# Buffers that outlive a stage: the first q and k, and the first y and inverses, loaded in the stage before

## The chip, the cores and the metric

The kernel runs on one core of one Trainium2 chip. Its engines are TensorE (PE, with its weight loads shown apart as PEld), VectorE (DVE), ScalarE (ACT), GpSimd (POOL) and SyncE (SP), which here issues nearly all transfers; ACT issues a few. The metric is the device time of one execution in microseconds. The time of the kernel before is the median of three executions.

## The reference

A transformer over x of shape (2, 2048, 256), 16 heads of 16:

```python
x = x + attn_a(layernorm(x))    # softmax times a causal decay table, then @ W_proj
x = x + ffn(layernorm(x))       # binarised weights, gelu, 256 -> 1024 -> 256
x = x + attn_b(layernorm(x))    # plain causal softmax, @ Wo + bo, then a layernorm with gamma, beta
x = x + ffn(layernorm(x))       # the same ffn again
```

Each attention forms q, k and v of every head, softmax(q k^T / 4) under a causal mask, and its product with v. `attn_a` multiplies the softmax by decay weights that depend on the distance of the two positions.

## The kernel before

The program is six stages, one behind the other: `setup` (signs and constants), `projections` named `qkv_a`, `attention` named `att_a`, `dense` named `mid` (projection of att_a, the ffn, and q, k, v of the second attention), `attention` named `att_b`, and `dense` named `end`. Each stage is a block: all engines meet at its end, its semaphores are cleared, and its buffers are given back. What one stage hands to the next goes through scratch tensors in DRAM: `qk` and `v` into an attention, `y` and `inverse` (the reciprocal softmax sums) into a dense stage. A stage's end waits for its own stores (the last `wait_ge` lines of its sync program).

A chunk is 512 positions, four (NC) for each of two batches; dense stages number them G = 0 to 7. An attention works on eight groups g of four heads, each with chunks c = 0 to 3.

**Attention.** `kop` and `qop` hold k and q of two groups (parities). Rows 0 to 63 of a chunk are four loads each of 16 rows, 128 KB (`load`, lines 616 to 632); rows 64 to 127 are padding, written by memsets (`pad`, line 601): VectorE fills the four chunks of `qop` of the first group and only then runs its PLAN (line 742), GpSimd fills the others. The q of group 0 is loaded by ACT (line 705), its k by SP (line 622). Then comes `va` (v, line 632). PLAN (`attention_plan`) is one list for all engines. It merges two streams by computed positions: items "M" (TensorE forms a score block in `pm`, line 829; VectorE takes its row maximum, lines 759 and 763) and items "S" (scores again, line 842; ScalarE takes exp, line 718), followed by "PO" and "PV" (sums and products with v). M runs ahead of S by a lead of 0.38 or 0.45 of a group. "MC" copies the maxima into row 64 of `qop` (line 652), "O" copies an output chunk out and gathers its sums (`scol`, line 661), and "SU" takes their reciprocal (line 809) and stores it. "L" items load the next group's q and k. Every engine takes its items strictly in the order of PLAN, and `pm` has four banks.

**Dense.** PLAN (`dense_plan`) is again one list. "Y": VectorE multiplies `y` by `inverse` (line 1324). "P": TensorE projects it (line 1179), VectorE adds x or bias. "S": moments and normalisation. In `end`, "A" and "N" add x and normalise once more. "X" transposes, "H" and "O" are the ffn. PLAN begins Y0, P0, S0, Y1, P1, S1, X0, H in `mid`, and Y0, P0, S0, Y1, A0, N0, P1, S1, X0, A1, N1, Y2, H in `end`. SP loads y(0), in `end` then bo, gamma and beta (line 1047), then y(1) and x(1), in `mid` then the weights; ACT loads the projection's weights, x(0) and the two sign matrices of 1 MB (lines 1244 to 1247). A y load is four transfers, two of y and two of inverse, 256 KB each.

## Time and profile before

| | us |
|---|---|
| median of three runs | 2675.54 (2669.0 to 2676.61) |
| profiled execution, its own time | 2671.95 |
| its span | 2670.2 |

By the timeline the stages of the profiled execution are:

| stage | from | to |
|---|---|---|
| setup | 0 | 34.0 |
| qkv_a | 34.0 | 147.3 |
| att_a | 147.3 | 1139.7 |
| mid | 1139.7 | 1466.0 |
| att_b | 1466.0 | 2413.7 |
| end | 2413.7 | 2670.2 |

Times in the rows are microseconds from the start of the span, unless marked ns. A timeline row is: start, duration, engine, source line, operation, output<-input, shapes, count, and in brackets the idle time of that engine before it and what released it. SPq and ACTq are the issue of a transfer by that engine, not the transfer.

### The profile page before, as it was taken

To read this page: it belongs to the slowest core of one execution; us is meant where nothing else is said; L and a number is where in the kernel's file an instruction comes from. 1 tells how busy PE (TensorE), PEld (TensorE's weight loads), DVE (VectorE), ACT (ScalarE), POOL (GpSimd) and SP (SyncE) were. 2 spreads that over 40 slices of the span, in tenths; PEclk is the share of its full clock that TensorE was granted. 3 is DMA by queue.
4 is the path that set the end of the run, shared out by engine and by line. 5 is a ranking of instruction groups with operands and counts; after the bars stand their busy time and mean duration, and the time that the engine had idled before them with its cause. 6 is when DMAs were issued, how large, how long until landed. Compare 5 with 4: busy or idle time off the path is not lost. (4 is left out here: it accounts for less than half of the span.)

```text
span 2670.2 us, 43926 instructions
## 1 busy us (share of the span) xinstructions
PE 2396.0 (90%) x13600; PEld 1367.6 (51%) x13600; DVE 1962.1 (73%) x4834; ACT 1499.8 (56%) x3293; POOL 1054.0 (39%) x1274
## 2 busy tenths in 40 slices
PE   4969999999999999859996899999999999992887
PEld 2544545555454545346764455555555555532666
DVE  5677888878888888337653988888888878833887
ACT  1218677776868777614331266666666666670233
POOL 0037778788787778813211301010010110103552
PEclk8969999999999999979998699999999999996999
DMA  4684243351615330053323644261542615004210
GB/s 150 255 145 59 37 55 51 45 73 18 85 26 66 46 50 10 10 164 115 130 98 123 88 65 62 30 85 30 66 61 30 85 26 70 10 9 140 77 50 32
DMA packets 158806, 188.69 MB, mean 71 GB/s; under 512 B 65520, under 2 KB 89584, under 8 KB 157808
## 3 DMA queue, kind: packets, MB, share of 16 engines
q1 hardware_dynamic: 153840, 175.91, 33.5%
q10 hardware_dynamic: 4736, 9.96, 1.9%
q8 instruction: 113, 1.85, 0.3%
q14 instruction: 117, 0.96, 0.2%
HBM read 114.37 MB, written 69.99 MB: 69 GB/s over the span
## 5 line engine op out<-in xcount | busy, mean ns | idle before, releaser
L688 POOL TENSOR_TENSOR att_a_wd<-att_a_wt,decay 128x256 f32<-128x256 f32 (+3 forms) x896 | 754.4, 872 | 208.5 <-PE att_a_po L864 120.5
L718 ACT ACTIVATE att_b_wt<-att_b_ps 128x512 f32<-128x512 f32 (+3 forms) x1280 | 592.3, 540 | 325.5 <-PE att_b_ps L842 323.7
L759 DVE TENSOR_REDUCE att_a_mpart<-att_a_pm 128x1 f32<-128x512 f32 x768 | 508.8, 686 | 115.9 <-PE att_a_pm L829 110.8
L759 DVE TENSOR_REDUCE att_b_mpart<-att_b_pm 128x1 f32<-128x512 f32 x768 | 503.5, 685 | 95.4 <-PE att_b_pm L829 93.7
L829 PE MATMUL att_a_pm<-att_a_kop,att_a_qop 128*128 128x512 f32 (+3 forms) x1280 | 510.8, 425 | 45.5 <-DMA att_a_kop<-qk 19.1
L718 ACT ACTIVATE att_a_wt<-att_a_ps 128x512 f32<-128x512 f32 (+3 forms) x896 | 433.0, 511 | 207.2 <-PE att_a_ps L845 145.0
L829 PE MATMUL att_b_pm<-att_b_kop,att_b_qop 128*128 128x512 f32 (+3 forms) x1280 | 486.7, 400 | 29.7 <-DMA att_b_kop<-qk 18.4
L842 PE MATMUL att_b_ps<-att_b_qop,att_b_kop 128*128 128x512 f32 (+3 forms) x1280 | 453.9, 384 | 13.7 <-DMA att_b_qop<-att_b_mrow 9.1
L698 POOL TENSOR_SCALAR_AFFINE_SELECT att_b_wt<-att_b_wt 128x512 f32<-128x512 f32 x128 | 81.4, 636 | 837.4 <-ACT att_b_wt L718 837.4
L829 PEld LDWEIGHTS att_a_pm<-att_a_kop,att_a_qop 128*128 128x128 f32 x1280 | 237.9, 193 | 307.2 <-DVE att_a_mpart L759 139.7
L829 PEld LDWEIGHTS att_b_pm<-att_b_kop,att_b_qop 128*128 128x128 f32 x1280 | 244.9, 194 | 245.9 <-DVE att_b_mpart L759 119.3
L842 PE MATMUL att_a_ps<-att_a_qop,att_a_kop 128*128 128x512 f32 (+3 forms) x896 | 319.4, 366 | 0.7 <-ACT att_a_wt L718 0.7
L842 PEld LDWEIGHTS att_b_ps<-att_b_qop,att_b_kop 128*128 128x128 f32 x1280 | 236.9, 189 | 131.2 <-ACT att_b_wt L718 80.9
L873 PE MATMUL att_b_po<-att_b_wt,att_b_va 128*17 128x512 f32 (+3 forms) x2560 | 296.4, 535 | 1.1 <-POOL att_b_wt L698 1.0
L724 ACT ACTIVATE att_a_pm<-att_a_pm,att_a_mpart 128x512 f32<-128x512 f32 x384 | 258.1, 673 | 69.3 <-DVE att_a_mpart L759 66.9
L763 DVE CUSTOM_DVE_ANT_0 att_a_pm<-att_a_pm,late 128x384 f32<-128x384 f32 (+3 forms) x512 | 248.4, 496 | 48.7 <-PE att_a_pm L829 47.2
L763 DVE CUSTOM_DVE_ANT_0 att_b_pm<-att_b_pm,late 128x384 f32<-128x384 f32 (+3 forms) x512 | 248.0, 497 | 43.7 <-PE att_b_pm L829 43.4
L842 PEld LDWEIGHTS att_a_ps<-att_a_qop,att_a_kop 128*128 128x128 f32 x896 | 169.9, 190 | 66.7 <-ACT att_a_wt L718 52.0
L859 PE MATMUL att_a_po<-att_a_wt,ones_strip 128*32 128x512 f32 (+3 forms) x1792 | 198.0, 513 | 1.8 <-ACT att_a_y L738 1.6
L864 PE MATMUL att_a_po<-att_a_wd,att_a_va 128*16 128x256 f32 (+3 forms) x1792 | 164.8, 440 | 2.9 <-POOL att_a_wd L688 2.8
L1262 ACT ACTIVATE end_g<-end_ph,b,alpha 128x512 f32<-128x512 f32 x64 | 50.0, 782 | 124.9 <-PE end_ph L1197 112.9
L845 PE MATMUL att_a_ps<-mask_k,identr 128*128 128x128 f32 x512 | 118.8, 236 | 0.0
(167 smaller groups left out, 2512.1 us busy)
## 6 DMA issues: line engine op xcount, KB each, us to landing
att_a_kop<-qk SPq DMA_DIRECT2D x128, 128.0 KB, 7.0
att_b_kop<-qk SPq DMA_DIRECT2D x128, 128.0 KB, 6.0
att_a_qop<-qk SPq DMA_DIRECT2D x112, 128.0 KB, 6.6
att_b_qop<-qk SPq DMA_DIRECT2D x112, 128.0 KB, 6.6
qk<-qkv_a_qk_hi SPq DMA_DIRECT2D x8, 1024.0 KB, 4.1
qk<-qkv_a_qk_lo SPq DMA_DIRECT2D x8, 1024.0 KB, 6.0
y<-att_a_y SPq DMA_DIRECT2D x32, 256.0 KB, 2.2
qk<-mid_qk_hi SPq DMA_DIRECT2D x8, 1024.0 KB, 4.3
```

The lines of the kernel that those rows point to most:

```text
L688: pool.tensor_tensor(wd[:, kq % 2, j, a:z], wt[:, kq % buffers, j, a:z], keep["decay"][:, u:u + z - a], ALU.mult).then_inc(w_decayed, 1)
L698: pool.affine_select(out=block, in_=block, compare_op=ALU.is_ge, fill=0.0, base=0, pattern=[[0, GH], [1, P]], channel_multiplier=-1).then_ ...
L718: act.activation(wt[:, kq % buffers, j, a:CH], pe_[:, n % EBANKS, 0:CH - a], ACT.Exp)\
L724: act.activation(pm[:, n % MBANKS, :], pm[:, n % MBANKS, :], ACT.Exp, bias=mpart[:, c, piece, u:u + 1], accum_out=fsum[:, c, piece, u:u + ...
L759: dve.tensor_reduce(mpart[:, c, piece, u:u + 1], pm[:, n % MBANKS, 0:w], AX.X, ALU.max, negate=True).then_inc(m_reduced, 1)
L763: dve.tensor_tensor_reduce(out=pm[:, n % MBANKS, 0:w], in0=pm[:, n % MBANKS, 0:w], in1=keep["late"][:, CH - w:CH], scale=-1.0, scalar=-2 * ...
L829: mm = pe.matmul(pm[:, n % MBANKS, 0:w], qop[:, par, c, j, qb * P:(qb + 1) * P], kop[:, par, j, piece * CH:piece * CH + w], start=True, st ...
L842: mm = pe.matmul(pe_[:, n % EBANKS, 0:CH - a], kop[:, par, j, kb * P:(kb + 1) * P], qop[:, par, c, j, a:CH], start=True, stop=not diagonal)
L845: mm = pe.matmul(pe_[:, n % EBANKS, 0:P], keep["identr"][:, :], keep["mask_k"][:, :], start=False, stop=True)
L859: pe.matmul(po[STRIP * j:STRIP * (j + 1), a:CH], keep["ones_strip"][:, :], wt[:, kq % buffers, j, a:CH], start=first, stop=False)
L864: mm = pe.matmul(po[STRIP * j:STRIP * j + VW, a:z], va[:, par, kb, j, :], wd[:, kq % 2, j, a:z], start=False, stop=last)
L873: mm = pe.matmul(po[STRIP * j:STRIP * j + VW, a:CH], va[:, par, kb, j, :], wt[:, kq % buffers, j, a:CH], start=first, stop=last)
```

## The change

Four buffers are allocated for the whole program: `k_first` and `q_first` (one chunk of k and of q with padding) and `y_first` and `inverse_first`. The attentions use the first two as the buffers of (parity 0, chunk 0), the dense stages the others as buffers of parity 0. The first contents of each are loaded in the stage in front: `load_first_chunk` (eight transfers of 128 KB) in qkv_a on SP ahead of the stores of the last chunk, and in `mid` on SP behind the last store of x; `load_y` (four transfers of 256 KB) in each attention on SP behind item ("SU", 6, 0). Each waits, by semaphores, for the stores that it reads. The next stage raises the matching semaphore itself in place of the load. `kop` and `qop` become one buffer per chunk. VectorE fills three paddings instead of four before its PLAN, GpSimd eleven instead of twelve; GpSimd fills those of the kept buffers in `setup`, and that of `q_first` again in `mid`. The end of each stage in front also waits for these loads.

```diff
--- before.py
+++ after.py
@@ constants @@
+FIRST_LOADS = 16 * 2 * PAIRS
+Y_LOADS = 16 * 2 * KT
@@ setup, gpsimd, behind the mask_k affine_select @@
+            pool.wait_ge(ident_ready, 4)
+            pool.memset(keep["k_first"][MROW:P, :, :].bitcast(F32), 1.0).then_inc(zeroed, 1)
+            pool.memset(keep["q_first"][MROW:P, :, :].bitcast(F32), 0.0).then_inc(zeroed, 1)
+            pool.wait_ge(zeroed, 8)
@@ projections, sync @@
                     if not last or c + 2 < NC:
                         load(b, c + 2)
+                    if last and c == NC - 1:
+                        sp.wait_ge(stored[0], STORE * (B * NC // 2))
+                        load_first_chunk(sp, keep, dram, first_in)
                     store(b, c)
...
                 sp.wait_ge(stored[par], STORE * (B * NC // 2 + 1))
+            sp.wait_ge(first_in, FIRST_LOADS)
@@ new functions @@
+def load_first_chunk(eng, keep, dram, loaded):
+    src = group_of(dram, 0)
+    for r in range(PAIRS):
+        rows = slice(r * HD, (r + 1) * HD)
+        eng.dma_start(keep["k_first"][rows, :, :].bitcast(F32), src[r % 2, 1, :, :, 0:CH]).then_inc(loaded, 16)
+        eng.dma_start(keep["q_first"][rows, :, :].bitcast(F32), src[r // 2, 0, :, :, 0:CH]).then_inc(loaded, 16)
+def load_y(eng, y, inverse, dram, b, c, loaded):
+    rows = dram["y"][b].rearrange("g (j s) t -> (g j) s t", s=STRIP)
+    for k in range(KT):
+        heads = slice(k * H // KT, (k + 1) * H // KT)
+        eng.dma_start(y[:, k, :], rows[heads, 0:HD, c * CH:(c + 1) * CH]).then_inc(loaded, 16)
+        eng.dma_start(inverse[:, k, :], dram["inverse"][b, c, heads, :].unsqueeze(1).to_broadcast([H // KT, HD, CH]))\
+           .then_inc(loaded, 16)
@@ attention @@
-        kop = sb("kop", [P, 2, GH, T], F32R)
-        qop = sb("qop", [P, 2, NC, GH, CH], F32R)
+        others = [(par, c) for par in range(2) for c in range(NC)][1:]
+        kop = {(0, 0): keep["k_first"], **{x: sb(f"kop{x[0]}{x[1]}", [P, GH, CH], F32R) for x in others}}
+        qop = {(0, 0): keep["q_first"], **{x: sb(f"qop{x[0]}{x[1]}", [P, GH, CH], F32R) for x in others}}
@@ attention, sync @@
-            for c in range(NC):
+            sp.sem_inc(qk_in[0][0], QK_LOADS)
+            for c in range(1, NC):
                 load(0, c)
...
+                if item == ("SU", GROUPS - 2, 0):
+                    sp.wait_ge(y_out[0], Y_DMAS * (NG * NC // 2 + 1))
+                    sp.wait_ge(s_out[0], 16 * (NG * NC // 2 + 1))
+                    load_y(sp, keep["y_first"], keep["inverse_first"], dram, 0, 0, first_in)
+            sp.wait_ge(first_in, Y_LOADS)
@@ attention, gpsimd @@
-            for t, par, padded in ((kop, 0, k_padded), (qop, 1, q_padded), (kop, 1, k_padded)):
-                pad(pool, t, par, padded[par])
-            pool.wait_ge(k_padded[1], NC)
+            pool.sem_inc(k_padded[0], 1)
+            pad(pool, kop, 0, range(1, NC), k_padded[0])
+            pad(pool, kop, 1, range(NC), k_padded[1])
+            pad(pool, qop, 1, range(NC), q_padded[1])
+            pool.wait_ge(q_padded[1], NC)
@@ attention, scalar @@
-            for c in range(NC):
+            for c in range(1, NC):
                 for r in range(PAIRS):
...
@@ attention, vector @@
-            pad(dve, qop, 0, q_padded[0])
             dve.sem_inc(m_reduced, MBANKS)
+            dve.sem_inc(q_padded[0], 1)
+            pad(dve, qop, 0, range(1, NC), q_padded[0])
@@ dense @@
-        y, x = sb("y", [P, 2, KT, CH], F32), sb("x", [P, 2, TB, D], F32)
-        inverse = sb("inverse", [P, 2, KT, CH], F32)
+        y, inverse = ([keep[f"{n}_first"], sb(f"{n}_second", [P, KT, CH], F32)] for n in ("y", "inverse"))
+        x = sb("x", [P, 2, TB, D], F32)
@@ dense, sync @@
-            load_y(0)
+            sp.sem_inc(y_in[0], Y_LOADS)
             if norm:
...
-            load_y(1)
+            load_y_of(1)
             load_x(1)
...
+                if item == ("Q", CHUNKS - 1, M - 1):
+                    sp.wait_ge(qk_out[0], STORE)
+                    load_first_chunk(sp, keep, dram, first_in)
                 if item == ("Q", G, M - 1):
...
+            if qkv:
+                sp.wait_ge(first_in, FIRST_LOADS)
@@ dense, gpsimd, with qkv @@
+                pool.wait_ge(power_ready, 1)
+                pool.wait_ge(vt_filled, 2)
+                pool.memset(keep["q_first"][MROW:P, :, :].bitcast(F32), 0.0).then_inc(vt_filled, 1)
+                pool.wait_ge(vt_filled, 3)
@@ build, keep @@
+            "k_first": sb("k_first", [P, GH, CH], F32R), "q_first": sb("q_first", [P, GH, CH], F32R),
+            "y_first": sb("y_first", [P, KT, CH], F32), "inverse_first": sb("inverse_first", [P, KT, CH], F32),
```

The matmuls and memsets otherwise only change how they name a buffer.

SP at the end of `qkv_a`, before. The names are DRAM scratch (`qk`, `v`) and buffers of the stage:

```order
L278 DMA v<-qkv_a_vt 128x1024
L276 DMA qk<-qkv_a_qk_hi 128x4x512
L276 DMA qk<-qkv_a_qk_lo 128x4x512
L278 DMA v<-qkv_a_vt 128x1024
L219 UNCONDITIONAL_BRANCH
L608 UNCONDITIONAL_BRANCH
L622 DMA att_a_kop<-qk 16x4x512 x16
L632 DMA att_a_va<-v 128x4x64 x4
```

The same place now, with the pair of k and q loads standing once of four times:

```order
L284 DMA v<-qkv_a_vt 128x1024
L545 DMA k_first<-qk 16x4x512
L546 DMA q_first<-qk 16x4x512
...
L282 DMA qk<-qkv_a_qk_hi 128x4x512
L282 DMA qk<-qkv_a_qk_lo 128x4x512
L284 DMA v<-qkv_a_vt 128x1024
L225 UNCONDITIONAL_BRANCH
L640 UNCONDITIONAL_BRANCH
```

Eight loads stand ahead of the last three stores of the stage, on the same queue.

SP at the start of `end`, before (the y and inverse pair stands once of two times):

```order
L1025 UNCONDITIONAL_BRANCH
L1034 DMA end_y<-y 128x1x512
L1035 DMA end_inverse<-inverse 128x1x512
...
L1047 DMA end_bo<-in_L_attn_b_bo 128x256
L1047 DMA end_gamma<-in_L_attn_b_gamma 128x256
L1047 DMA end_beta<-in_L_attn_b_beta 128x256
```

The same place now; the y here is that of G = 1:

```order
L1066 UNCONDITIONAL_BRANCH
L1081 DMA end_bo<-in_L_attn_b_bo 128x256
L1081 DMA end_gamma<-in_L_attn_b_gamma 128x256
L1081 DMA end_beta<-in_L_attn_b_beta 128x256
L554 DMA end_y_second<-y 128x1x512
L555 DMA end_inverse_second<-inverse 128x1x512
```

The four transfers of y(0) are gone from the head of the queue, and y(1) has moved up.

VectorE at the start of `att_a`, before and now:

```order
L606 MEMSET att_a_qop 64x2048 x4
L744 MEMSET att_a_po 128x512
L745 MEMSET att_a_mneg 128x128
L746 MEMSET att_a_scol 128x64
```

```order
L638 MEMSET att_a_qop 64x2048 x3
L785 MEMSET att_a_po 128x512
L786 MEMSET att_a_mneg 128x128
L787 MEMSET att_a_scol 128x64
```

One memset of four has left VectorE's program there.

## Rows read from the trace of the kernel before

**Rows 1.** The page, part 1: busy time of each engine.

```profile
PE 2396.0 (90%) x13600; PEld 1367.6 (51%) x13600; DVE 1962.1 (73%) x4834; ACT 1499.8 (56%) x3293; POOL 1054.0 (39%) x1274
```

**Rows 2.** Waits: waiter, releaser, us in total, times, longest.

```profile
PE att_a_pm L829 <- DMA att_a_kop<-qk: 19.1, 2, 16.4
PE att_b_pm L829 <- DMA att_b_kop<-qk: 18.4, 2, 17.4
DVE end_yt L1324 <- DMA end_inverse<-inverse: 21.0, 1, 21.0
DVE mid_yt L1324 <- DMA mid_inverse<-inverse: 20.9, 1, 20.9
```

**Rows 3.** Timeline, start of att_a.

```profile
147.79 1.76 DVE L606 MEMSET att_a_qop<- 64x2048 f32 x1 [5.00 <-PEq L70]
...
154.21 1.76 DVE L606 MEMSET att_a_qop<- 64x2048 f32 x1 [0.38 <-issue]
...
156.98 0.11 DVE L749 MEMSET att_a_ftotal<- 128x64 f32 x1
...
157.75 0.45 PE L829 MATMUL att_a_pm<-att_a_kop,att_a_qop 128*128 128x128 f32 x1 [16.42 <-DMA att_a_kop<-qk]
...
158.36 0.30 DVE L763 CUSTOM_DVE_ANT_0 att_a_pm<-att_a_pm,late 128x128 f32<-128x128 f32 x1 [1.27 <-PE att_a_pm L829]
...
167.12 0.69 DVE L759 TENSOR_REDUCE att_a_mpart<-att_a_pm 128x1 f32<-128x512 f32 x1 [1.23 <-PE att_a_pm L829]
```

**Rows 4.** Timeline, start of att_b.

```profile
1466.50 1.76 DVE L606 MEMSET att_b_qop<- 64x2048 f32 x1 [5.82 <-PEq L70]
...
1475.49 0.11 DVE L746 MEMSET att_b_scol<- 128x64 f32 x1
...
1477.24 0.30 DVE L763 CUSTOM_DVE_ANT_0 att_b_pm<-att_b_pm,late 128x128 f32<-128x128 f32 x1 [1.64 <-PE att_b_pm L829]
```

**Rows 5.** Timeline, start of mid.

```profile
1157.58 1.23 DVE L1324 TENSOR_TENSOR mid_yt<-mid_y,mid_inverse 128x1024 f32<-128x1024 f32 x1 [20.87 <-DMA mid_inverse<-inverse]
...
1158.95 6.22 PE L1179 MATMUL mid_pp<-mid_wp,mid_yt 128*128 128x256 f32 x16 [27.25 <-DVE mid_yt L1324]
...
1169.97 0.80 PE L1179 MATMUL mid_pp<-mid_wp,mid_yt 128*128 128x256 f32 x1 [4.80 <-DVE mid_yt L1324]
```

**Rows 6.** Timeline, start of end.

```profile
2431.69 1.23 DVE L1324 TENSOR_TENSOR end_yt<-end_y,end_inverse 128x1024 f32<-128x1024 f32 x1 [20.97 <-DMA end_inverse<-inverse]
...
2433.03 2.35 POOL L1116 TENSOR_TENSOR end_xb<-end_x,end_beta 128x1024 f32<-128x1024 f32 x1 [19.23 <-DMA end_beta<-in_L_attn_b_beta]
...
2443.62 5.41 PE L1179 MATMUL end_pp<-end_wp,end_yt 128*128 128x256 f32 x16 [4.80 <-DVE end_yt L1324]
...
2449.47 1.23 DVE L1347 TENSOR_TENSOR end_x<-end_zg,end_xb 128x1024 f32<-128x1024 f32 x1 [5.90 <-POOL end_zg L1124]
...
2452.95 1.23 DVE L1332 TENSOR_TENSOR end_z<-end_pp,end_bo 128x1024 f32<-128x1024 f32 x1
```

**Rows 7.** Windows: the first row names the columns.

```profile
core 0: us, PE busy (x) PEld busy (x) DVE busy (x) ACT busy (x) POOL busy (x), PEclk, DMA share, GB/s
136.00:139.40 3.40, 3.40 (x13) 2.26 (x12) 1.38 (x2) 1.20 (x2) 0.00 (x0) 1.00 0.03 11
139.40:146.40 7.00, 1.93 (x9) 1.35 (x8) 1.42 (x4) 0.00 (x0) 0.00 (x0) 0.79 0.95 375
166.60:184.00 17.40, 16.39 (x36) 9.22 (x36) 16.85 (x51) 0.00 (x0) 1.72 (x1) 0.61 1.11 131
188.00:200.00 12.00, 10.96 (x35) 8.17 (x34) 10.29 (x26) 7.83 (x20) 4.31 (x4) 0.58 0.99 120
1440.50:1457.00 16.50, 12.77 (x31) 6.74 (x32) 2.72 (x4) 3.78 (x5) 2.38 (x6) 0.69 0.01 1
2216.00:2230.00 14.00, 14.00 (x90) 8.32 (x86) 11.64 (x25) 9.85 (x23) 1.81 (x3) 1.00 0.97 117
```

**Rows 8.** Timeline of VectorE at item ("SU", 6, 1) of att_b.

```profile
2231.09 0.35 DVE L809 RECIPROCAL att_b_inverse<-att_b_scol 128x32 f32<-128x32 f32 x1
```

More of the change, by code:

```diff
@@ L245, in projections @@
         hi_ready, lo_ready, v_kept, vt_filled = sm("hi_ready"), sm("lo_ready"), sm("v_kept"), sm("vt_filled")
-        stored = [sm(f"stored{i}") for i in range(2)]
+        stored, first_in = [sm(f"stored{i}") for i in range(2)], sm("first_in")
         block = ctx.enter_context(nc.Block())
@@ L564, in attention @@
         pv_done, o_kept = sm("pv_done"), sm("o_kept")
[L565 removed]
+        y_out, first_in = [sm(f"y_out{i}") for i in range(2)], sm("first_in")
         block = ctx.enter_context(nc.Block())
[L568 to L569 removed]
+        qk_g = [group_of(dram, g) for g in range(GROUPS)]
         v_g = [[dram["v"][g // NG, c][:, 0:TB * H * VW].rearrange("p (t g e) -> g p t e", t=TB, g=NG)[g % NG]
@@ L1026, in _, with load_y_of @@
         def _(sp):
[L1027 to L1028 removed]
+            def load_y_of(G):
                 if G >= 2:
                     sp.wait_ge(yt_ready, G - 1)
[L1031 to L1037 removed]
+                load_y(sp, y[G % 2], inverse[G % 2], dram, G // NC, G % NC, y_in[G % 2])
             def load_x(G):
```

47 lines of the change are left out of this document (18 added, 29 removed).

## The prediction

> **What bounds the kernel now.** I read the page first. TensorE is busy for 90% of the span and VectorE for 73% [rows 1], so inside a stage a few us of transfer more or less hardly show. The change acts where one stage ends and the next begins, and there the table of waits is the view to read. It names four waits at the heads of stages: TensorE waits 19.1 us for k and q in att_a and 18.4 us in att_b, VectorE waits 20.9 us for y and inverse in mid and 21.0 us in end [rows 2]. They add up to 79 us, or 3% of the time, and that is what a quick reading would promise. It is not what can be gained. For each I went to the timeline and asked what is late next once this transfer is there; then I looked at the windows for what the queue is doing where the transfer is moved to.
>
> **att_a, the start.** VectorE does not stand still while k is on its way. It fills four paddings, the first from 147.79, the fourth from 154.21 [rows 3], so one costs (154.21 - 147.79) / 3 = 2.14 us, and then a few small ones until 156.98 + 0.11 = 157.09. Its first maximum begins at 158.36 after an idle time of 1.27 us. So behind a wait of TensorE of 16.4 us VectorE had only 1.27 us to give. The change takes one padding away: VectorE is free at 157.09 - 2.14 = 154.95, TensorE has filled its four banks long before, and the first maximum moves from 158.36 to 154.95, or 3.4 us. The wait for k is replaced by VectorE's paddings. The second part of the wait is chunk 1: VectorE idled 1.23 us ahead of 167.12. Chunk 1 now stands first in the queue, where chunk 0 stood, so it lands by 157.75 and is wanted only after sixteen maxima, at about 162. That idle time goes, about 1.1 us of it. Together 4.5 us. From there to the first S the stream of maxima is bound by VectorE: it is busy 16.85 of 17.4 us between 166.6 and 184 [rows 7], so what it starts earlier arrives earlier. Bounds: 3.4 (chunk 1 is still late) to 5.0.
>
> **att_b, the start.** The same reading: the small memsets end at 1475.49 + 0.11 = 1475.60, less 2.14 is 1473.46, against the first maximum at 1477.24 [rows 4]. That is 3.7 us after a few hundredths of start; bounds 3.4 to 4.0.
>
> **mid, the start.** Y0 is free at once, P0 follows when its weights are there, and S0. But PLAN has Y1 next on VectorE and P1 ahead of X0 on TensorE, so X0 and everything behind it wait for y(1). Before, y(0) was first in SP's queue and was there at 1157.58 [rows 5]; y(1) came later and P1 began at 1169.97. Now y(1) is first in the same queue, of the same size, beside the same megabytes on ACT's queue. It lands when y(0) landed, at 1157.58, and P1 begins where P0 began, at 1158.95. The gain is 1169.97 - 1158.95 = 11.0 us and not 20.9. Bounds: 10, if the sign matrices hold it a little longer, to 16, if y(1) came so early that only P0 counted.
>
> **end, the start.** Again y(1) takes the place of y(0) as the thing that is late, but here bo, gamma and beta now stand ahead of it. In the kernel before they were behind y(0) and the last of them was there 2433.03 - 2431.69 = 1.3 us after it [rows 6]. In the other order the sum is the same, so y(1) lands at about 2433.0. Y1 ends at 2434.3 and P1 begins at 2434.4 against 2443.62. A0, which stands behind Y1 on VectorE, began at 2449.47; it now begins at 2434.4 too, 15.1 us earlier, since GpSimd's part of S0 has ended by then. P1 takes 5.4 us and then releases what VectorE did at 2452.95: 2434.4 + 5.5 = 2439.9, or 13.0 us earlier. Behind this both chains join, and I take 14.0; bounds 12 to 16.
>
> A rule of the Trainium skill bears on both places. The page DMA: Bandwidth & Descriptors, section Why a DMA increments its semaphore by 16 and not by 1, says that a transfer runs on the largest number of engines, up to 16, that divides the slowest dimension of both its sides. A y transfer has eight heads there, so by the rule all of y(1) goes through eight engines, the same ones that y(0) used. If it were spread over all sixteen, y(1) would come earlier and mid would move towards its bound of 16. The rows cannot tell the two apart, because y(0) was loaded in the same form.
>
> **qkv_a, the end.** This is what the move costs. SP issues the eight loads behind the v store of the last chunk but one, and the three last stores stand behind them on the same queue. Loads of this form move 120 GB/s while the engines of the queue are busy 0.99 of the time (188 to 200) [rows 7], so eight of 131 KB, 1.05 MB, take 8.7 us. The queue has a hole of 3.4 us there, 136.0 to 139.4 at a share of 0.03, and from 139.4 to 146.4 the stores fill it at 375 GB/s and the stage ends 0.9 us behind them. The hole hides 3.4 us; 8.7 - 3.4 = 5.3 us are late at the end of the stage. Bounds: 0, if stores pass the loads, to 8.7, if the loads start late.
>
> The Trainium skill speaks against the change here. SBUF — State Buffer, section Door 1, says that bandwidth depends on how many of 16 ports the partitions reach, four for the 16 rows of one such load, at 27.2 GB/s each. By that 109 GB/s the estimate for the 1.05 MB would be 9.6 us and the term 6.2. The row has 120, so I stay with 5.3.
>
> **mid, the end.** The same loads follow the last store of x. From 1440.5 to 1457.0 the queue is idle at a share of 0.01 [rows 7]: 16.5 us for 8.7 us of work. Cost 0; without the cover it would be 8.7.
>
> **The y loads in the attentions.** Four transfers, 1.05 MB, ahead of the loads ("L", 7, 2), the gather ("O", 6, 1) and all that SP issues behind them. Where they stand nobody waits for them, but the gather of the sums is queued behind. In att_b the queue is at 0.97 from 2216 to 2230 [rows 7], and VectorE's reciprocal at 2231.09 just does not wait [rows 8]. The load is 2.8 us of queue at 375 GB/s and 8.7 at 120. What VectorE waits, TensorE rides out for as long as its banks hold scores. In att_a the queue is less tight at that item. I take 1.5 us for both together; bounds 0 and 8.7.
>
> **At no cost.** GpSimd's two new memsets in setup and the one in mid should take the 1.76 us of VectorE's, which have the same form [rows 3], and lie in its idle head of the stage. The waits for `stored[0]`, `qk_out[0]`, `y_out[0]` and `s_out[0]` ask for stores of batch 0 or of chunks long landed. Fewer issues on SP and ACT release nobody.
>
> **The sum.** -4.5 - 3.7 - 11.0 - 14.0 + 5.3 + 1.5 = -26.4 us. Against the profiled execution's own 2671.95 that is 2645.6. The median of the runs is 3.6 us above that execution, so against it the forecast is 2675.54 - 26.4 = 2649.1, rounded 2649.
>
> **The rivals.**
> (a) The displaced transfers cost nothing: the stores overlap with the loads and the y loads find gaps. For it: reads and writes need not share one limit. Against it: one queue, and a share of 0.99. -26.4 - 6.8 = -33.2, 2642.
> (b) y(1) is not late in the dense stages, and P0 is what counts: mid gives 16 and end 16. For it: 1 MB less in the queue. Against it: that megabyte stood behind, not ahead. -26.4 - 5 - 2 = -33.4, 2642.
> (c) The attentions give back what they gain: the first S hangs on the last transfers of the head and not on VectorE, so the starts give 0, and each y load costs 5. -25 + 5.3 + 10 = -9.7, 2666.
> (d) The change does not do what it says: TensorE still waits at the head, for the pads or for chunk 1 at the old place. Then both attention terms fall: -18.2, 2657.
> (e) Slower than before. TensorE's granted clock is 0.58 to 0.61 of full in the head of att_a and 1.00 in its middle [rows 7], the two levels being 1.2 and 2.4 GHz. A stage that starts with a burst of short work and then waits may stay at the lower level when the steady part begins. At 1.2 GHz a stretch in which TensorE is always busy takes twice as long, so a stretch that took 26.4 us at 2.4 GHz pays the whole gain away, and 40 us of such stretches give 2649 + 40 = 2689. It decides from 26.4 us on. Against it: the change shortens the idle heads and adds none.
>
> **The chances.** Forecast 0.52, (a) 0.17, (b) 0.11, (c) 0.11, (d) 0.05, (e) 0.04. A measurement of this kernel tells about 0.3%, or 8 us, from no change. Forecast, (a), (b), (d) and most of (c) are faster by more: 0.90, and of (c) the part with dearer y loads is within: 0.06. Slower keeps 0.04. The range must take in (a), (b) and (d), at 2642 to 2657, with the bounds of the terms: the early side goes to 2637, since qkv_a's term can be 0 together with one of the dense stages at its bound, and the late side to 2661, between (d) and (c).
>
> **What would show it.** In the profile after: no wait of TensorE for k at the head of an attention, but its maxima start some 7.6 us after the stage's start and right behind the three paddings; a wait of VectorE for `inverse_second` in mid that ends about 18 us after the stage's start, and in end about 19 us; DMA busy at about 120 GB/s in the last us of qkv_a ahead of the stores, and that stage longer by 5.3 us; in att_b the reciprocal of ("SU", 6, 1) waiting. The prediction is wrong if y(1) is there before S0 has ended, if the stores of qkv_a end on time, or if the first S of an attention does not move with the first maximum.

## The result, and the profile after

| | before | after |
|---|---|---|
| median of four runs | 2676.07 (2669.0 to 2677.01) | 2659.24 (2657.27 to 2662.01) |
| profiled execution, its own time | 2671.95 | 2657.27 |
| its span | 2670.2 | 2655.5 |

The ratio is 0.9944, 95% interval 0.9931 to 0.9957: faster by 0.56%; the medians lie 16.8 us apart, the two profiled executions 14.7. The forecast was 26.4 us. The sign was right, the size was not, and the time lies inside the range, near its late end.

The page of the changed kernel hardly differs in the busy times [rows 1]:

```profile
PE 2400.0 (90%) x13600; PEld 1368.4 (52%) x13600; DVE 1955.7 (74%) x4832; ACT 1496.9 (56%) x3293; POOL 1053.1 (40%) x1275
```

So I went by stages. A stage starts with its first instruction in the timeline, and the table has the length of each and what the prediction had put into it:

| stage | before | after | difference | forecast |
|---|---|---|---|---|
| setup | 34.0 | 33.8 | -0.2 | 0 |
| qkv_a | 113.3 | 118.2 | +4.9 | +5.3 |
| att_a | 992.4 | 990.4 | -2.0 | -4.5 and a part of +1.5 |
| mid | 326.3 | 315.8 | -10.5 | -11.0 |
| att_b | 947.7 | 954.1 | +6.5 | -3.7 and a part of +1.5 |
| end | 256.5 | 243.3 | -13.3 | -14.0 |
| sum | 2670.2 | 2655.5 | -14.7 | -26.4 |

Four of the six are where they were expected. The gap of 11.7 us is in the attentions, nearly all of it in att_b, and it is not at their starts.

**The starts.** The timeline of VectorE at the start of att_a, which begins at 151.94, answers to [rows 3]; the row of ACT is the issue of the other chunks' q:

```profile
151.94 6.23 ACTq L745 DMA_DIRECT2D att_a_qop<-qk  x12
...
152.62 1.76 DVE L638 MEMSET att_a_qop<- 64x2048 f32 x1 [10.61 <-PEq L72]
154.76 1.76 DVE L638 MEMSET att_a_qop<- 64x2048 f32 x1 [0.38 <-issue]
156.90 1.76 DVE L638 MEMSET att_a_qop<- 64x2048 f32 x1 [0.38 <-issue]
...
159.81 0.30 DVE L804 CUSTOM_DVE_ANT_0 att_a_pm<-att_a_pm,late 128x128 f32<-128x128 f32 x1
```

Three paddings in a row, a few small fills, and then the first maximum without an idle time, 7.9 us after the stage's start; before, it was 158.36 - 147.30 = 11.1. In att_b it is 7.7 against 1477.24 - 1466.01 = 11.2, a gain of 3.6.

TensorE still waited at the head of att_a, but not for k; of all it waited for, this row is that place:

```profile
PE att_a_pm L870 <- ACTq L748: 17.9, 1, 17.9
```

ACT releases `f_done` behind its twelve issues, at 158.3. It cost nothing, since VectorE was free only at 159.8. What stands behind the maxima moved with them: the first exp of an S item comes 43.1 us after the stage's start in att_a instead of 47.7, and 46.0 in att_b instead of 49.6.

In the two dense stages the waits for `inverse` of 20.9 and 21.0 us [rows 2] have become these (waiter, releaser, us in total, times, longest):

```profile
PE end_pp L1222 <- DMA end_wp<-in_L_attn_b_Wo: 12.7, 1, 12.7
PE mid_pp L1222 <- DMA mid_wp<-in_L_attn_a_W_proj: 11.1, 1, 11.1
POOL end_xb L1159 <- DMA end_beta<-in_L_attn_b_beta: 10.1, 1, 10.1
DVE end_yt L1367 <- DMA end_inverse_second<-inverse: 5.8, 1, 5.8
DVE mid_yt L1367 <- DMA mid_inverse_second<-inverse: 5.5, 1, 5.5
```

The first two look large, but the idle time of TensorE from the stage in front is in them: P0 of mid begins at 1145.88, 3.6 us after the stage's start. What counts is y(1), in the timeline of mid and of end:

```profile
1142.32 0.45 ACTq L1287 DMA_DIRECT2D mid_wp<-in_L_attn_a_W_proj  x1
...
1160.45 1.23 DVE L1367 TENSOR_TENSOR mid_yt<-mid_y_second,mid_inverse_second 128x1024 f32<-128x1024 f32 x1 [5.51 <-DMA mid_inverse_second<-inverse]
...
1161.73 6.07 PE L1222 MATMUL mid_pp<-mid_wp,mid_yt 128*128 128x256 f32 x16 [10.39 <-DVE mid_yt L1367]
```

```profile
2412.25 0.11 POOL L1122 MEMSET end_power<- 128x4 f32 x1 [8.23 <-POOLq L72]
...
2433.04 1.32 DVE L1367 TENSOR_TENSOR end_yt<-end_y_second,end_inverse_second 128x1024 f32<-128x1024 f32 x1 [5.83 <-DMA end_inverse_second<-inverse]
...
2434.42 6.31 PE L1222 MATMUL end_pp<-end_wp,end_yt 128*128 128x256 f32 x16 [10.80 <-DVE end_yt L1367]
```

y(1) is there 18.1 us after mid's start. P1 begins 19.4 us after it; y(0)'s place before the change was 1158.95 - 1139.72 = 19.2 [rows 5]. In `end`, which starts at 2412.25 (before at 2413.69), y(1) is there after 20.8 us and P1 begins after 22.2, where it began after 29.9 before.

**att_b, the middle.** Here is what is new. The timeline of VectorE around item ("SU", 6, 1) answers to [rows 8], where there was no idle time, and the timeline of TensorE lies beside it:

```profile
2218.96 0.14 DVE L804 DVE_READ_ACCUMULATOR2_ANT att_b_mpart<- 128x1 f32 x1
2229.98 0.35 DVE L850 RECIPROCAL att_b_inverse<-att_b_scol 128x32 f32<-128x32 f32 x1 [10.88 <-DMA att_b_scol<-att_b_y]
2230.25 1.82 DVE L800 TENSOR_REDUCE att_b_mpart<-att_b_pm 128x1 f32<-128x512 f32 x3
```

```profile
2221.11 1.05 PE L914 MATMUL att_b_po<-att_b_wt,att_b_va 128*17 128x512 f32 x8
2230.93 0.80 PE L870 MATMUL att_b_pm<-k_first,att_b_qop 128*128 128x512 f32 x1 [8.77 <-DVE att_b_mpart L800]
```

VectorE stands 10.88 us for the gathered sums. TensorE goes on for 3.1 us more, until 2222.16, and then stands 8.77 us for a maximum. Compared instruction by instruction with the kernel before, VectorE is 12.2 us ahead just in front of this place and 1.6 us ahead just behind it: 10.6 us are lost at one item. (Both numbers are from the start of the span.) The windows show the transfers there (the columns are those of [rows 7]):

```profile
2199.00:2222.00 23.00, 23.00 (x140) 12.26 (x138) 16.83 (x38) 16.67 (x37) 2.54 (x4) 1.00 0.99 122
2222.00:2230.00 8.00, 0.17 (x4) 0.00 (x0) 0.02 (x1) 0.00 (x0) 0.00 (x0) 0.67 0.44 67
```

While everyone waits for a transfer, the DMA engines are busy for 0.44 of the time and move 67 GB/s. That is not a full queue, and it needed an explanation.

### The profile page after: what moved, and what is told of

The parts are those of the page before. It is cut to its first block and busy times, and to the rows that moved or that the text cites. A ratio compares the mean times of both kernels' runs of the same rounds, so it can differ in the third digit from the quotient of the medians.

```text
span 2655.5 us, 43935 instructions
## 1 busy us (share of the span) xinstructions
PE 2400.0 (90%) x13600; PEld 1368.4 (52%) x13600; DVE 1955.7 (74%) x4832; ACT 1496.9 (56%) x3293; POOL 1053.1 (40%) x1275
## 5 line engine op out<-in xcount | busy, mean ns | idle before, releaser
L870 PE MATMUL att_a_pm<-att_a_kop,att_a_qop 128*128 128x512 f32 (+3 forms) x1024 | 404.8, 414 | 19.3 <-ACT att_a_pm L764 12.0
L870 PE MATMUL att_b_pm<-att_b_kop,att_b_qop 128*128 128x512 f32 (+3 forms) x1024 | 383.2, 387 | 8.1 <-DVE att_b_mpart L800 4.2
L883 PE MATMUL att_b_ps<-att_b_qop,att_b_kop 128*128 128x512 f32 (+3 forms) x1024 | 359.8, 382 | 9.3 <-DMA att_b_qop<-att_b_mrow 4.6
L870 PEld LDWEIGHTS att_a_pm<-att_a_kop,att_a_qop 128*128 128x128 f32 x1024 | 188.2, 191 | 231.3 <-DVE att_a_mpart L800 116.4
L870 PEld LDWEIGHTS att_b_pm<-att_b_kop,att_b_qop 128*128 128x128 f32 x1024 | 194.2, 191 | 169.5 <-DVE att_b_mpart L800 88.6
L883 PE MATMUL att_a_ps<-att_a_qop,att_a_kop 128*128 128x512 f32 (+3 forms) x768 | 272.3, 364 | 0.8 <-ACT att_a_wt L758 0.8
L883 PEld LDWEIGHTS att_b_ps<-att_b_qop,att_b_kop 128*128 128x128 f32 x1024 | 189.6, 189 | 105.0 <-ACT att_b_wt L758 69.0
L883 PEld LDWEIGHTS att_a_ps<-att_a_qop,att_a_kop 128*128 128x128 f32 x768 | 145.1, 190 | 59.8 <-ACT att_a_wt L758 47.6
```

The costliest lines, as they stand in the source:

```text
L870: mm = pe.matmul(pm[:, n % MBANKS, 0:w], qop[par, c][:, j, qb * P:(qb + 1) * P], kop[par, piece][:, j, 0:w], start=True, stop=True)
L883: mm = pe.matmul(pe_[:, n % EBANKS, 0:CH - a], kop[par, kb // TB][:, j, kb % TB * P:(kb % TB + 1) * P], qop[par, c][:, j, a:CH], start=Tru ...
```

## The experiments

Theory: the y load stands in SP's queue ahead of the gather of ("O", 6, 1) and costs att_b 10.6 us; the rest of the forecast holds. Rivals: the wait comes from the attention's new alignment; or the part on q and k has cost it. Medians and ratios below are each against runs of the kernel before made beside them.

### The two parts apart

```
# e1_qk_alone: no load_y in the attentions; at the head of mid and end
-            sp.sem_inc(y_in[0], Y_LOADS)
+            load_y_of(0)
# e2_y_alone: no load_first_chunk; at the head of the attentions
-            for c in range(1, NC):
+            for c in range(NC):
                 load(0, c)
```

> The change without its part on y and the inverses: nothing is loaded for the dense stages in an attention, y(0) stands first in SP's queue at the head of mid and end again. The first q and k stay as the change has them. Theory (the y load delays the gather of the sums in att_b): the wait of VectorE for scol that ends at L850 near 2230 us, 10.9 us in the changed kernel, is gone; att_b is shorter than in the changed kernel by 10 to 11 us, mid is longer by 10.5 and end by 13.3, each as long as before the change. The profiled span is 2655.5 + 13.2 = 2669, the median 2672, the ratio to before 0.998 to 1.000. Rival (the wait comes from the attention's new alignment or a lower clock, and not from the load): the wait stays, att_b stays at 954, the median is 2683 and slower than before.

Measured: 2671.9, ratio 0.999 (0.998 to 1.0), span 2670.9. The reciprocal of ("SU", 6, 1) waits for nothing, att_b has 946.5 us, mid 327.2, end 257.6. **The part on q and k alone is worth about nothing**: of the gains at the starts of the attentions 3.7 us are left in att_a as a whole and 1.2 in att_b, qkv_a pays 4.1, and mid and end are each 1 us longer than before. The 1.2 is from a single profiled execution, and the part on the lower clock below shows that such a number in att_b is uncertain by some 6 us.

> The change without its part on q and k: chunk 0 of group 0 is loaded at the head of each attention again, as before the change; the paddings stay where the change put them, and so do the y loads. Theory: att_a begins 5.0 to 5.5 us earlier after qkv_a's last store than in the changed kernel, and its first maximum comes when k has landed, about 10.5 us after the stage's start; att_b still has the wait of 10 to 11 us for scol. Sum against before: -10.5 (mid) - 13.3 (end) + 10.6 (att_b) + 0 to 1 for the rest, about -13, so a median of 2662 to 2664 and a ratio of 0.995. Rival (the y loads cost nothing and the q and k part costs the 11 us): the wait for scol is gone and the median is 2652.

Measured: 2663.22, ratio 0.9959 (0.9945 to 0.9973), as forecast. The wait for the sums is there again, with 11.58 us, so it belongs to the y load. The first maximum of att_a comes 12.4 us after the stage's start and not 10.5: with VectorE's paddings done by 153.6 it idled 4.6 us for k.

### The y load at another place

```
# e3_y_in_group_7
-                if item == ("SU", GROUPS - 2, 0):
+                if item == ("SU", GROUPS - 1, 0):
```

> The changed kernel with one line moved: y and inverse are loaded behind the item (SU, 7, 0) instead of (SU, 6, 0), in both attentions. SP's queue is idle there (share of DMA time 0.05 from 2310 to 2330 in the changed kernel). Theory: the wait for scol at (SU, 6, 1) in att_b goes from 10.9 us to under 0.5 and the gather of (O, 7, 1), which is 14 us behind the load, does not wait; the span falls by 10 to 11 us, the median is 2649 and the ratio to before 0.990. Rival (the wait has another cause): it stays, and the median stays at 2659. Second rival (the cost only moves with the load, to a gather of group 7): the wait for scol appears at (SU, 7, 1) and the median is 2655 to 2659.

Measured: 2651.73, ratio 0.9915 (0.9901 to 0.9928), span 2645.5, which is 10.0 us less than that of the changed kernel. att_b has 941.5 us instead of 954.1, VectorE has no idle time at ("SU", 6, 1), and the cost does not turn up at ("SU", 7, 1). The theory holds, both rivals fall. The window in which this kernel moves its y load, with nothing else in the queue:

```profile
2310.50:2317.00 6.50, 6.50 (x45) 3.44 (x37) 4.41 (x11) 3.98 (x13) 1.91 (x3) 1.00 0.46 159
```

The load is over within 6.5 us, at a busy share of 0.46. Why then did it cost 10.9 in group 6? Three kernels ask that.

```
# e5_half_of_y: k = 0 behind ("SU", 6, 0), k = 1 behind ("SU", 7, 0)
+                    load_y(sp, keep["y_first"], keep["inverse_first"], dram, 0, 0, first_in, [item[1] - GROUPS + 2])
# e6_y_on_the_other_queue: the same item, in ACT's program
+                    load_y(act, keep["y_first"], keep["inverse_first"], dram, 0, 0, first_in)
# e9_y_behind_the_loads
-                if item == ("SU", GROUPS - 2, 0):
+                if item == ("L", GROUPS - 1, 2):
```

> The changed kernel with half of the y load moved: the first 128 columns' y and inverse (k = 0, two transfers, 0.52 MB) stay behind (SU, 6, 0), the other half goes behind (SU, 7, 0). A dose for the wait of 10.9 us. Theory (the wait is the queue time of the bytes that stand ahead of the gather, with no slack in front): the wait for scol at (SU, 6, 1) in att_b is half, 5.0 to 6.0 us, and the median lies half way between the changed kernel's 2659 and the 2652 to 2649 of the whole load in group 7, at 2655. Rival (a fixed cost of having these transfers in the queue, by their form or by the issues, and not by their bytes): the wait stays near 10 us or is gone altogether.

Measured: the wait is 6.93 us, not 5 to 6, and the median 2655.21, ratio 0.993 (0.9911 to 0.9948). The dose counts, but not in proportion.

> The changed kernel with the same y load at the same item, (SU, 6, 0), issued by ACT on its own DMA queue instead of by SP. Theory A (the cost is the order in SP's queue: the gather of the sums stands behind the y load): with the load in another queue the gather only shares the engines with it; the two loads of 1.05 MB on SP's queue are slowed by less than the load's whole time, the wait falls from 10.9 us to between 2 and 6, and the median is 2652 to 2656. Theory B (the cost is the bytes, whichever queue they stand in, since the DMA engines are busy 0.97 of the time): the wait stays at 9 to 11 us and the median at 2659. Theory C (the port or engine limit of SP's loads leaves room for the y load beside them): the wait is under 1 us and the median 2650. ACT's own four issues are 2.5 us of an engine that is busy for two thirds of the time there.

Measured: the wait is 8.15 us, the median 2657.84. None of the three was right. Three quarters of the wait stay although the gather no longer stands behind the y load in its queue. So the gather's place behind the load in SP's queue is at most a quarter of it, and a full queue is not the cause either: in the wait the share is 0.42.

> The changed kernel with the y load behind the item (L, 7, 2) instead of (SU, 6, 0): it stays ahead of the same gather, in the same queue, and only changes places with the nine transfers of (L, 7, 2). It asks why 1.05 MB that took 6.6 us alone in group 7 cost a wait of 10.9 us here. In the changed kernel the DMA share falls to 0.44 and 67 GB/s in the 8 us in which VectorE and TensorE stand, from 2222 to 2230. Theory (half of the DMA engines carry the y load, its transfers have eight heads; the other half runs ahead with (L, 7, 2), and when it is done the first half has those packets still to move, alone): with no other transfer between y and the gather that tail goes, and the wait is what the y load takes alone, 5.4 to 6.6 us, less the slack of 0.7: 4.7 to 6. The median is 2654. Rival (the bytes cost the same wherever they stand, 1.05 MB at 92 to 120 GB/s): the wait stays between 8 and 11 us, and the median at 2657 to 2659.

Measured: the wait is 5.66 us, with the same transfers ahead of the same gather, and only the order of two groups of them turned. VectorE is not simply later here: from the first issue of the k and q loads of ("L", 7, 1) to the reciprocal it is 32.9 us in the changed kernel and 27.6 in this one. The windows of this kernel, and below them those of the changed kernel over the same transfers:

```profile
2217.00:2222.00 5.00, 5.00 (x30) 2.25 (x28) 4.55 (x10) 4.24 (x9) 0.00 (x0) 1.00 1.12 120
2222.00:2230.00 8.00, 6.02 (x36) 3.12 (x32) 2.42 (x5) 4.13 (x8) 0.00 (x0) 1.00 0.56 157
```

```profile
2206.00:2217.00 11.00, 11.00 (x71) 6.46 (x68) 9.17 (x21) 7.67 (x18) 1.20 (x2) 1.00 1.10 110
2217.00:2222.00 5.00, 5.00 (x30) 2.40 (x28) 2.10 (x5) 4.05 (x8) 0.00 (x0) 1.00 0.61 141
2222.00:2228.00 6.00, 0.17 (x4) 0.00 (x0) 0.00 (x0) 0.00 (x0) 0.00 (x0) 0.72 0.55 75
```

With the loads of k and q first, they run at 1.12 and 120 GB/s until they are through, then the y load at about half the share and at 157 GB/s. With the y load first, the share falls to about half as early as 2218, 11 us before the last of these loads has landed, and from 2222 on only 75 GB/s move. What they move can be told from the rises of the semaphores, which the trace keeps one by one. A load of k or q raises its semaphore 16 times as its parts land, a y transfer 8 times (and once right after its issue). In the changed kernel the nine transfers of ("L", 7, 2) land half, 72 of 144 rises, from 2209.3 to 2218.8, and the other half from 2222.3 to 2229.3; the y load, issued ahead of them, lands from 2212.8 to 2221.8 but for one rise at 2223.4. In the kernel with the loads first, all 144 rises come between 2214.8 and 2223.7 and those of y behind them, to 2229.9. The gather raises its semaphore four times per transfer as it lands, all of them behind 2228.7 in the changed kernel, so it uses engines of the half that is late.

That is the mechanism which the order of the two decides: the y load keeps one half of the engines busy, the other half goes on with the next k and q transfers, and when y is through, the first half still has its own part of them to move, alone. The overlap saves nothing. With y first, y takes 12.9 us beside the other half's loads (2208.9, when the loads in front have landed, to 2221.8) and the late half of the loads another 7.5, together 20.4. With the loads first, they take 8.6 us on all engines (2215.1 to 2223.7) and y 6.2 alone, together 14.8. In e6_y_on_the_other_queue the nine transfers land in two halves as well, 72 rises up to 2220.2 and 72 from 2222.8 to 2229.0. It fits that the other queue helped so little: the gather needs engines of that half whichever queue the y load stands in. I read a part as the share of one engine, since the busy share halves where only eight parts are left; the trace does not name the engines.

The rule for it stands in the Trainium skill, page DMA: Bandwidth & Descriptors, section Why a DMA increments its semaphore by 16 and not by 1: a transfer's engines are the largest number up to 16 that divides the slowest dimension of both sides, which gives eight for eight heads. The trace agrees: the shares are 0.46 alone and 0.44 in the wait, and each y transfer lands in eight parts.

The median of this kernel, 2656.64, did not follow its wait, though. The 5.2 us won there were lost earlier in att_b of the profiled execution, as the part on the lower clock shows.

### The loads at the end of qkv_a

```
# e4_two_loads_a_chunk
-                    if last and c == NC - 1:
-                        sp.wait_ge(stored[0], STORE * (B * NC // 2))
-                        load_first_chunk(sp, keep, dram, first_in)
+                    if last:
+                        if c == 0:
+                            sp.wait_ge(stored[0], STORE * (B * NC // 2 - 1))
+                        load_first_chunk(sp, keep, dram, first_in, [c])
```

> The changed kernel with the eight loads at the end of qkv_a spread: two of them, a k and a q, in each of the last sequence's four chunks, ahead of that chunk's stores, in place of all eight in the last chunk. Two loads are 2.2 us at 120 GB/s; the queue is idle for 1.5 to 2 us in each chunk of 11.85 us and for 4.5 us ahead of the last stores. Theory (the loads keep the last stores waiting in one queue, and only what does not fit into the hole shows): the start of att_a comes 4.5 to 5.5 us earlier, nothing else moves, and the median is 2654. Rival (stores and loads overlap, and the 5.5 us are the end of the stage waiting for something else): att_a starts where it does in the changed kernel, and the median is 2659. Second rival (the earlier loads delay stores and then PE through the double buffers): qkv_a's chunks grow by 1 us each and the median is 2657.

Measured: 2653.11, ratio 0.992 (0.9902 to 0.9937). qkv_a has 112.6 us instead of 118.2. From the last v that VectorE writes in it to the first instruction of att_a it is 4.5 us, as before the change, and 9.9 in the changed kernel: 5.4 us, the theory, and within 0.1 us the term of the prediction. The windows of the changed kernel and of this one, ahead of and behind the last stores:

```profile
137.00:139.50 2.50, 2.50 (x13) 2.22 (x12) 0.69 (x1) 0.60 (x1) 0.00 (x0) 1.00 1.09 124
139.50:145.00 5.50, 1.05 (x5) 0.57 (x4) 1.42 (x4) 0.00 (x0) 0.00 (x0) 1.00 1.07 200
145.00:152.00 7.00, 0.00 (x0) 0.00 (x0) 0.00 (x0) 0.00 (x0) 0.00 (x0) 0.57 0.69 273
```

```profile
136.00:139.00 3.00, 3.00 (x13) 2.28 (x12) 1.14 (x2) 0.60 (x1) 0.00 (x0) 1.00 0.30 96
139.00:142.00 3.00, 1.25 (x6) 0.76 (x4) 1.42 (x4) 0.00 (x0) 0.00 (x0) 1.00 1.05 408
142.00:146.00 4.00, 0.00 (x0) 0.00 (x0) 0.00 (x0) 0.00 (x0) 0.00 (x0) 0.92 0.72 288
```

In the first the loads move 124 GB/s at a full share and the stores, at some 400 GB/s when alone, come behind them.

### What bounds the start of an attention

```
# e7_paddings: q chunks 2 and 3 of parity 0
-            pad(dve, qop, 0, range(1, NC), q_padded[0])
+            pad(dve, qop, 0, [1], q_padded[0])
# in GpSimd's program, behind k's chunk c
+                if c > 1:
+                    pool.wait_ge(q_padded[0], c)
+                    pad(pool, qop, 0, [c], q_padded[0])
# and ACT: e_weights and f_done released ahead of its twelve issues
# e11_later_maxima, ahead of VectorE's paddings
+            for k in range(5):
+                dve.memset(extra[:, :], 0.0).then_inc(extra_done, 1)
+                dve.wait_ge(extra_done, k + 1)
```

> The changed kernel with the paddings of q's chunks 2 and 3 of parity 0 filled by GpSimd instead of VectorE, and with ACT's two releases (e_weights, f_done) ahead of its twelve issues instead of behind. It measures what bounds the start of the attentions now. Theory (VectorE's paddings, 2.14 us each): the first maximum begins 4.3 us earlier in both attentions, 3.5 us after the stage's start instead of 7.7; chunk 1, wanted 7.3 us later, has landed or is at most 1 us late. The median is 2659 - 6 to 8.6, so 2651 to 2653. Rival (the transfers of chunk 1 are what is late next): VectorE waits 2 to 4 us ahead of the first maximum of chunk 1, what is gained at the first maximum is lost there, and the median is 2657 to 2659.

Measured: the first maximum comes 3.5 us after the start in att_a and 3.3 in att_b, 4.35 us earlier in each, and VectorE idles ahead of chunk 1, for 1.7 us in att_a and 1.0 in att_b. The median is 2656.95, ratio 0.9937 (0.9918 to 0.9956), some 2 us under the changed kernel, and the intervals of the two ratios overlap. So the first maxima did what the theory said, but the median is the one that the rival forecast. Part of the gain went at chunk 1; and in the profiled execution att_b, 7.9 us ahead of the kernel before at its first maximum, was 2.4 ahead in front of the y load's place, mostly by losses at the boundaries of its groups.

> The changed kernel with five small fills more on VectorE at the head of each attention, ahead of its paddings, each waited for: some 0.4 to 0.6 us each, so 2 to 3 us by which its first maximum comes later. Two questions. First, whether VectorE sets the start of the attentions: by that theory each attention's first maximum is 2 to 3 us later and the attention longer by the same less the slack at chunk 1 (0), together 4 to 6 us; rival: something else is late and it costs under 1 us. Second, the short stretches of low granted clock at the boundaries of the groups (in the changed kernel at 707 and 827 us of att_a and 224 and 906 of att_b, 3.4 us each; in the kernel with the y load behind the loads at 224, 340, 565, 773 and 906 of att_b): if they depend on where the boundaries fall in time and not on the work, they turn up at other boundaries here although nothing behind the head is changed, and the stage's length changes by 1 to 2 us for each, beyond the 2 to 3. Median by the first theory alone 2663 to 2665; with the second anything from 2659 to 2669.

Measured: 2665.71, ratio 0.9966 (0.9954 to 0.9978). Both first maxima come 2.6 us later and att_a is longer by 3.0. What VectorE has to do ahead of its first maximum sets the start: taking work away brought it forward and adding work put it off. att_b is longer by 6.0, and its other 3 us are the subject of the next part.

### Short stretches at the lower clock

Every attention ends a group and begins the next some 112 to 121 us later. At some of these boundaries the granted clock falls to the lower of its two levels, 1.2 instead of 2.4 GHz, for a few us. The same boundary of att_a, first in the kernel before, then in the changed one:

```profile
856.00:862.00 6.00, 4.29 (x33) 2.37 (x31) 5.19 (x22) 2.26 (x7) 4.02 (x5) 1.00 0.02 3
```

```profile
856.00:862.00 6.00, 4.29 (x20) 2.07 (x20) 3.97 (x17) 1.37 (x4) 3.11 (x4) 0.78 0.01 2
```

And a boundary of att_b in the changed kernel and in e9_y_behind_the_loads (there 4 us later), each with the window in front of it:

```profile
2012.00:2018.00 6.00, 5.15 (x42) 2.60 (x41) 4.61 (x21) 3.01 (x11) 1.30 (x3) 1.00 0.02 3
2018.00:2024.00 6.00, 5.20 (x34) 3.23 (x33) 4.70 (x17) 3.89 (x8) 0.60 (x1) 1.00 0.01 1
```

```profile
2016.00:2022.00 6.00, 5.12 (x42) 2.66 (x34) 4.17 (x21) 2.39 (x9) 1.90 (x3) 1.00 0.02 4
2022.00:2028.00 6.00, 3.87 (x17) 2.86 (x18) 3.01 (x9) 2.39 (x4) 0.00 (x0) 0.72 0.00 0
```

TensorE is busy for 5.15 and 5.12 of the 6 us in front, the work is the same, and the clock falls in one and not in the other. In the changed kernel two boundaries of att_a have such a stretch where the kernel before has none; by the starts of VectorE's instructions 1.4 us are lost at each, and that is the larger part of the 3 us that att_a loses behind its start. In att_b, in front of the y load's place, they stand at these boundaries, in us from the stage's start: 565 before the change; 224 in the changed kernel; 224, 340 and 565 with the y load behind the loads; 340 and 565 in e11_later_maxima; 220, 449 and 561 in e7_paddings. The kernel e11 differs from the changed one at the stage's head alone, and its stretches lie elsewhere.

It would be natural to conclude that the place of the boundaries in time decides. The profiles contradict that, as far as time from the start of the span is meant. e3_y_in_group_7 and e9_y_behind_the_loads run the same program in att_b up to the loads of group 7. It starts at 1458.66 and 1458.70, and up to the boundary at 224 VectorE's instructions lie within 0.2 us of each other. Then e3 has one stretch, at 224, and e9 three. In front of the y load's place e3 is 5.3 us ahead of the kernel before and e9 1.0 us behind it, counted from the stage's start: 6.3 us of difference without a difference in the program there. Those two ran on different chips, but e5_half_of_y and e6_y_on_the_other_queue ran on one, are the same in att_b up to ("SU", 6, 0), and have their stretches at 224, 452 and 565 the one and at 336 the other. What decides it at one boundary was not settled, and no kernel has two profiles here; I take it as chance in a single comparison.

### The edits together

> Three edits of the runs so far in one kernel: y and inverse loaded behind (SU, 7, 0), two of the first loads of q and k in each chunk of qkv_a's last sequence, and the two paddings on GpSimd with ACT's releases first. If the gains lie in different places they add: against the changed kernel's 2659 the first gave 8 to 10 us, the second 6, the third is expected at 6 to 8.6. Expected median 2636 to 2640, ratio to before 0.986 to 0.988. If the third gives nothing: 2644.

Measured: 2638.46, ratio 0.9871 (0.9851 to 0.9891), span 2636.7.

> The y load in group 7 and two first loads a chunk in qkv_a, together, without the edit to the paddings. The kernel with all three edits had a median of 2638.5. Theory (the paddings are worth what they are worth at the first maximum less what chunk 1 then gives back, about 2.5 us in each attention): this one is 4 to 6 us above it, at 2643 to 2645, ratio to before 0.989. Rival (the paddings are worth nothing in the sum, since the first S or the group's first boundary takes it back): 2638 to 2640.

Measured: 2644.46, ratio 0.9882 (0.9863 to 0.99). The gains add, and the paddings, worth 2 us on the changed kernel, are worth 6 here, 3.4 in att_a and 5.0 in att_b by the stages of the profiled executions. The low-clock stretches are a part of such differences in a profiled execution, so the split between the stages is not firm.

```
# e12_signs_behind_y, on top of e8_all_moved, in ACT's program at the head of mid and end
+            act.wait_ge(y_in[1], Y_LOADS)
             act.dma_start(w1s[:, :, :].bitcast(F32), dram["w1s"]).then_inc(signs_in, 16)
             act.dma_start(w2s[:, :, :].bitcast(F32), dram["w2s"]).then_inc(signs_in, 16)
```

> The kernel with all three edits and a fourth: ACT issues the two loads of the sign matrices (1 MB each) at the heads of mid and end only when y(1) has landed. It asks what makes y(1) land 18 us after the stage's start when the same load took 6.6 us alone. Theory (its 2 KB packets wait behind the 8 KB packets of the sign matrices on the same engines): y(1) lands 9 to 11 us after the start, P1 follows P0 without a pause, X0 and the first H come up to 8 us earlier unless the sign matrices, 2 MB at 350 GB/s, are late then; mid and end are each 3 to 8 us shorter, and the median is 2638 - 6 to 16, most likely 2628. Rival (the signs are late next, or y(1) is slow by its own form and the 9 loads around it): y(1) still lands at 15 us or later, or the first H waits for the sign matrices, and the median is 2636 to 2642.

Measured: 2630.87, ratio 0.9847 (0.9832 to 0.9862), the best of all. The timeline of mid in this kernel, which starts at 1134.17:

```profile
1147.19 1.23 DVE L1373 TENSOR_TENSOR mid_yt<-mid_y_second,mid_inverse_second 128x1024 f32<-128x1024 f32 x1 [0.46 <-DMA mid_inverse_second<-inverse]
...
1159.41 0.80 PE L1245 MATMUL mid_ph<-mid_xt_hi,mid_w_signs 128*128 128x512 f32 x1 [4.57 <-DMA mid_w_signs<-w2s]
```

y(1) is there 13.0 us after the start instead of 18.5, between the two theories; then the first H waits 4.57 us for the sign matrices, as the rival said. Against e8_all_moved mid is 6.6 us shorter and end 7.4, while att_b, where nothing was changed, is 3.7 longer in this execution; the median gains 7.6 and not 14. A part of y(1)'s time was the sign matrices, and they are what is late next.

## Why the prediction was right and wrong

**Right: mid, the start.** "Now y(1) is first in the same queue ... It lands when y(0) landed": P1 begins 19.4 us after the stage's start where the prediction had 19.2, and mid is 10.5 us shorter against 11.0. Reading which wait ends last, and not adding up the waits, was what made this right.

**Right in size, not in its parts: end, the start**, 13.3 us against 14.0. The forecast had P1 at 2434.4 and it began at 2434.42, but that is luck: the stage started 1.4 us earlier than the one of the kernel before, from which the forecast was worked out. From the stage's start y(1) was there after 20.8 us and not 19.3, P1 began after 22.2 and not 20.7, and z(1) after 28.5 and not 26.2, since P1 took 6.3 us and not 5.4. The granted clock over P1 was 0.58 where it had been 0.68 before. P1 gained 7.8 us and z(1) 10.7, where the forecast had 9.2 and 13.0. What made the stage come out near 14 is the other chain: A0 began 13.7 us earlier (forecast 15.1), and the first H on TensorE 14.0.

**Right: qkv_a, the end.** Loads at 120 GB/s, a hole of 3.4 us, 5.3 us late. Spreading the loads gave back 5.4 us. Rival (a) needed the stores to pass the loads, and they did not. By the Trainium skill's SBUF — State Buffer, section Door 1, the estimate was 109 GB/s and 6.2 us; this kernel's windows have 124, so the row was the better source.

**Right: both starts of the attentions**, by VectorE's paddings. The stream of maxima came 5.0 and 3.6 us earlier and the first exp 4.5 and 3.6, against a forecast of 4.5 and 3.7. The two runs that moved the first maximum both ways show that the bound is there.

**Wrong: the y loads in the attentions.** The step was "What VectorE waits, TensorE rides out for as long as its banks hold scores ... I take 1.5 us for both together; bounds 0 and 8.7." The place was right, and the reciprocal that "just does not wait" was named. But it was on the edge: whatever is added to the queue in front of it is waited for in full, 10.88 us. TensorE rode out 3.1 us at its end of it, and even so the loss was 10.6 us. A likely reason, which no run tested, is that VectorE is itself busy for 0.83 of the time here [rows 7] and cannot make up for a wait. The value should have been taken near the upper end. And the upper end was too low: 8.7 us was the price of such bytes at the rate of a full queue, while the load, 6.5 us alone, costs 11 where transfers on all engines stand behind it. The prediction had the rule for the number of engines in its hands, used it for mid, and did not apply it to the same transfers in the attention.

**Not foreseen: the low-clock stretches.** Most of 3 us in att_a; in att_b they differ from one execution to the next. Rival (e) was about the clock, but at the heads of the stages, and its 40 us did not come.

The working, with the y loads at 10.6 and att_a's stretches at 3, would be -26.4 - 1.5 + 10.6 + 3 = -14.3, against -14.7 measured; the other terms are off by up to 0.7 us either way and cancel. Rival (c) had the mechanism, in part: it let each y load cost 5, and the starts give nothing, which was wrong. In att_a the y load, issued at the same item, cost nothing that shows: the reciprocal of ("SU", 6, 1) comes 33 us behind the load's issue there, and 17 us behind it in att_b.

## What to carry to other kernels

When a transfer is moved into a stage that is busy, look at each wait behind it in its queue that ends at zero now: it has no slack, and here an added wait of 10.88 us cost 10.6. Count a transfer on half of the engines as a cost to every transfer behind it, and put it where the queue is empty, or last before a pause. A gain at the head of a stage is to be sought by asking what is late next, and here the moves were worth about their forecast once the transfers had a free place: without its two costs it is -33.2 us, and e10_two_moved lies 32.0 under the kernel before.

## What the runs showed of the hardware

The y load of 1.05 MB took 6.5 us at a share of 0.46 and 159 GB/s alone, cost 5.66 us of wait right ahead of the gather, 8.15 from another queue, and 10.88 with the nine transfers of a k and q chunk behind it. Each of its transfers landed in eight parts, those of k and q in 16, and the late eight parts of each of the nine landed up to 2229.3, when the early ones had been there by 2218.8. Loads of 16 rows moved 120 to 124 GB/s at a full share, stores of all rows about 400. And at places where TensorE is busy for 5.1 of 6 us its granted clock may fall to the lower level or not, for the same work, at some 1.4 us a time or more.
